# Digraph mixes as products of fp16 halves, delta turned by a transfer, and VectorE operands held in PSUM

## The reference

```
u     = h @ h.T / sqrt(384)
delta = softmax(u) * adj
attn  = delta / (delta.sum(-1) + 1e-10)
ctx   = (attn * upper) @ (h @ Wl.T + bl) + diag(attn)[:, None] * (h @ Ws.T + bs) + (attn * lower) @ (h @ Wr.T + br)
h     = relu((ctx - mean) / sqrt(var + 1e-12) * g + beta)
```

## Time and profile before

| | |
|---|---|
| median of 3 runs | 2729.16 us (2726.61 to 2732.68) |
| profiled execution, its own time | 2730.39 us |
| its span, first to last instruction | 2728.5 us |
| PE busy | 2582.3 us (95%) |
| POOL, DVE, ACT busy | 2117.1 (78%), 2077.7 (76%), 2046.5 us (75%) |
| mean granted TensorE clock | 0.986 |

### The profile page before, as it was taken

The page is one execution under the profiler, slowest core; times in us unless marked ns, Lnnn a source line. Parts: engine busy times, 40 slices in busy tenths (PEclk is TensorE's granted clock), DMA queues, the critical chain, the costliest instruction groups (busy, mean ns, idle before and its releaser), DMA issues.

```text
span 2728.5 us, 90881 instructions
## 1 busy us (share of the span) xinstructions
PE 2582.3 (95%) x33728; PEld 1930.4 (71%) x33728; DVE 2077.7 (76%) x7848; ACT 2046.5 (75%) x5716; POOL 2117.1 (78%) x3211
## 2 busy tenths in 40 slices
PE   5899999999999999999999999999999999999995
PEld 4667777776777777777777777777777777777763
DVE  6677877777877777777777777777787777887774
ACT  6667777777777777777777777777777777787775
POOL 6577878778778788778787788888787787887774
PEclk9899999999999999999999999999999999999997
DMA  7734544445444544444454454444454544454433
GB/s 182 164 62 78 90 86 83 91 84 93 81 87 80 91 91 80 90 91 80 87 94 80 88 93 80 90 91 79 88 94 84 86 88 79 85 96 82 78 61 74
DMA packets 809952, 243.18 MB, mean 89 GB/s; under 512 B 768688, under 2 KB 808752, under 8 KB 809520
## 3 DMA queue, kind: packets, MB, share of 16 engines
q1 hardware_dynamic: 801056, 222.42, 45.5%
q10 hardware_dynamic: 8464, 14.94, 1.8%
HBM read 35.92 MB, written 12.58 MB: 18 GB/s over the span
## 4 chain that ended last, share of the span: by engine, by line
PE 45%; POOL 18%; DVE 16%; ACT 7%; DMA 6%; issue 6%; SPq 1%; DVEq 0%; POOLq 0%; ACTq 0%
PE bank L921 7%; PE bank L923 6%; PE bank L922 6%; PE bank L912 5%; PE bank L913 5%; PE bank L914 5%; DMA region<-region 5%; POOL region L717 3%; DVE region L1091 3%; POOL ab L733 3%; PE bank L995 3%; ACT region L832 2%; POOL region L706 2%; PE bank L951 2%; POOL region L733 2%
## 5 line engine op out<-in xcount | busy, mean ns | idle before, releaser
L912 PE MATMUL bank<-region,w_hi 128*128 128x128 f16 x3960 | 686.0, 220 | 35.0 <-DMA region<-region 25.0
L913 PE MATMUL bank<-region,w_hi 128*128 128x128 f16 x3960 | 685.6, 220 | 0.0
L914 PE MATMUL bank<-region,w_lo 128*128 128x128 f16 x3960 | 685.4, 220 | 0.0
L921 PE MATMUL bank<-w_hi,region 128*128 128x384 f16 x1815 | 593.9, 327 | 11.4 <-DMA region<-region 6.1
L923 PE MATMUL bank<-w_hi,region 128*128 128x384 f16 x1815 | 593.2, 327 | 0.0
L922 PE MATMUL bank<-w_lo,region 128*128 128x384 f16 x1815 | 593.1, 327 | 0.0
L717 POOL TENSOR_TENSOR region<-region 128x512 f16<-128x512 f32 x330 | 385.2, 1167 | 220.6 <-ACT region L838 219.2
L832 ACT ACTIVATE region<-region,small 128x128 f32<-128x128 f32 x1320 | 419.8, 390 | 133.1 <-DVE small L1091 73.2
L912 PEld LDWEIGHTS bank<-region,w_hi 128*128 128x128 f16 x3960 | 390.0, 98 | 63.3 <-issue 26.4
L1091 DVE CUSTOM_DVE_ANT_0 region<-bank,mask 128x128 f32<-128x128 f32 x1320 | 304.4, 285 | 134.5 <-PE bank L951 123.2
L913 PEld LDWEIGHTS bank<-region,w_hi 128*128 128x128 f16 x3960 | 389.9, 98 | 23.8 <-issue 16.5
(11 more groups left out here) (229 smaller groups left out, 7795.8 us busy)
## 6 DMA issues: line engine op xcount, KB each, us to landing
region<-region SPq DMA_TRANSPOSE x715, 3.1
last_unit<-w_dram ACTq DMA_DIRECT2D x19, 576.0 KB, 6.0
x<-x_dram SPq DMA_DIRECT2D x55, 192.0 KB, 2.5
out_dram<-region SPq DMA_DIRECT2D x55, 192.0 KB, 2.2
adj<-adj_dram SPq DMA_DIRECT2D x55, 64.0 KB, 2.3
mask<-adj_t_dram SPq DMA_DIRECT2D x55, 64.0 KB, 2.0
rows<-rows_dram ACTq DMA_DIRECT2D x5, 576.0 KB, 4.3
last_unit<-last_unit SPq DMA_TRANSPOSE x117, 3.1
```

The source lines that it names most:

```text
L912: pe.matmul(dst, lhsT=w_hi[:, w, k, cols], rhs=t_hi[u][:, k, :], start=(k == 0), stop=False)
L913: pe.matmul(dst, lhsT=w_hi[:, w, k, cols], rhs=t_lo[u][:, k, :], start=False, stop=False)
L914: last = pe.matmul(dst, lhsT=w_lo[:, w, k, cols], rhs=t_hi[u][:, k, :], start=False, stop=(k == DT - 1))
L921: pe.matmul(dst, lhsT=t_hi[u][:, k, :], rhs=w_hi[:, w, k, :], start=(k == 0), stop=False)
```

## The change

- Delta: `delta_di` writes its product into the second quarter of the same bank that holds u. `sums` makes the reciprocal of the row sum (a power of -1) in place of the column of 1e-12. ScalarE `delta` writes delta x reciprocal as fp16 into SBUF (the high half), VectorE `delta_low` writes the rest as fp16 (the low half), and takes the diagonal from the bank. The bank is held until then.
- The turn: SP starts a DMA transpose of both halves (128x256 fp16), and POOL `turn_delta` multiplies the turned halves by the two triangles in one instruction (128x512 fp16 out). PE's transpose and VectorE's triangles go.
- The sides: projections 9, 11, 12, 14 go the way that q and k of layer 0 go: VectorE `add_bias` from PSUM into `z` with the bias row, ScalarE a high fp16 half, POOL `low` the low half. POOL `bias` remains for 10 and 13 (the self term). The right side's `add_bias` waits for the left side's `low`, as both use `z`.
- `mix` 2 and 3: six fp16 matmuls of 384 columns each in place of two in fp32.
- Operands of VectorE: `u_gcn` masks left into SBUF and right in its bank, and adds those; `divide` keeps its reciprocals, and for layer 0 also its result, in the last attention bank, from which `residual` 0 reads; a column of `inner` 0 and 1 moves into the mix bank. The attention banks of steps 2 and 5 are so held until `residual` 0 and `divide` 1.
- `PERIOD`, `SHIFTED` and the wished times in `PARTS` are new, so the order of parts on every engine is another one.

```diff
-PERIOD = 20.1080
+PERIOD = 22.1046
...
-    (PE, "mix", 2): (-138.244, 1.340, 1.570, ((VECTOR, "turn_delta", 0), (POOL, "bias", 9), (POOL, "bias", 10), (POOL, "bias", 11)), ()),
...
-           "u_di": lambda k: (VECTOR, "delta_di", k), "turn_delta": lambda k: (VECTOR, "turn_delta", k),
+           "u_di": lambda k: (VECTOR, "delta_low", k),
...
+            def delta_turn(i, layer):
+                u = i % UNITS
+                sp.wait_ge(*mixed_out.at(i, "low delta", layer))
+                sp.dma_start_transpose(delta_t[u], delta_hl[u].rearrange("p a n -> p (a n)")).then_inc(landed.of(i), 16)
...
-                pool.tensor_scalar(col(u, EPS), col(u, DENOM), col(u, DENOM), 1e-12, ALU.mult, ALU.mult).then_inc(gpsimd_done.of(i), 1)
+                pool.tensor_tensor(col(u, INVERSE), col(u, DENOM), constant(MINUS_ONE), ALU.pow).then_inc(gpsimd_done.of(i), 1)
+
+            def turn_delta(i, layer):
+                u = i % UNITS
+                pool.wait_ge(*landed.at(i, "delta", layer))
+                pool.tensor_tensor(triangles[u], delta_t[u].unsqueeze(1).broadcast_to([128, 2, 2, N]),
+                                   tri[:, :, :].unsqueeze(2).broadcast_to([128, 2, 2, N]), ALU.mult).then_inc(gpsimd_done.of(i), 1)
...
+            def high_delta(i, layer):
+                u = i % UNITS
+                act.wait_ge(*gpsimd_done.at(i, "row scale", layer))
+                act.activation(delta_hl[u][:, 0, :], delta_of(i, layer), ACT.Copy, scale=col(u, INVERSE)).then_inc(scalar_done.of(i), 1)
...
-                    pe.matmul(made[:, 0:D], lhsT=triangles[u][:, 0, :], rhs=proj[u][0], start=True, stop=False)
-                    pe.matmul(made[:, 0:D], lhsT=triangles[u][:, 1, :], rhs=proj[u][2], start=False, stop=True)\
-                      .then_inc(multiplied.of(i), 1)
+                    dst = made[:, 0:D]
+                    for side, w in enumerate((left, right)):
+                        high, low = (triangles[u][:, side, n, :] for n in range(2))
+                        h = side_of(u, w)
+                        pe.matmul(dst, lhsT=high, rhs=h[:, 0, :], start=(side == 0), stop=False)
+                        pe.matmul(dst, lhsT=high, rhs=h[:, 1, :], start=False, stop=False)
+                        last = pe.matmul(dst, lhsT=low, rhs=h[:, 0, :], start=False, stop=(side == 1))
+                    last.then_inc(multiplied.of(i), 1)
...
+                    if w in SIDES[1::2]:
+                        dve.wait_ge(*low_of_shifted.at(i, "made", w - 2))
...
-                dve.tensor_tensor(u_pair[u], bank("u_gcn", layer, i)[:, 0:2 * N].rearrange("p (a n) -> p a n", n=N), mask_pair[u], ALU.mult)\
-                   .then_inc(numbers.of(i), 1)
-                dve.wait_ge(*numbers.at(i, "masked", layer))
-                dve.tensor_tensor(e_of(i, "u_gcn", layer), u_pair[u][:, 0, :], u_pair[u][:, 1, :], ALU.add).then_inc(mixed_out.of(i), 1)
+                left, right = (bank("u_gcn", layer, i)[:, n * N:(n + 1) * N] for n in range(2))
+                dve.tensor_tensor(u_left[u], left, mask_pair[u][:, 0, :], ALU.mult).then_inc(numbers.of(i), 1)
+                dve.tensor_tensor(right, right, mask_pair[u][:, 1, :], ALU.mult).then_inc(numbers.of(i), 1)
+                dve.wait_ge(*numbers.at(i, "right masked", layer))
+                dve.tensor_tensor(e_of(i, "u_gcn", layer), right, u_left[u], ALU.add).then_inc(mixed_out.of(i), 1)
...
-                dve.tensor_tensor_reduce(out=score[u][:, 2, :], in0=turned, in1=ident, scale=1.0, scalar=0.0, op0=ALU.mult,
-                                         op1=ALU.add, accum_out=col(u, DIAGONAL)).then_inc(numbers.of(i), 1)
-                dve.tensor_tensor(triangles[u], turned.unsqueeze(1).broadcast_to([128, 2, N]), tri[:, 0:2, :], ALU.mult)\
+            def delta_low(i, layer):
+                u = i % UNITS
+                dve.wait_ge(*scalar_done.at(i, "high delta", layer))
+                dve.scalar_tensor_tensor(delta_hl[u][:, 1, :], delta_of(i, layer), col(u, INVERSE), delta_hl[u][:, 0, :], ALU.mult, ALU.subtract)\
                    .then_inc(mixed_out.of(i), 1)
+                dve.tensor_tensor_reduce(out=delta_of(i, layer, 2), in0=delta_of(i, layer), in1=ident, scale=col(u, INVERSE), scalar=0.0,
+                                         op0=ALU.mult, op1=ALU.add, accum_out=col(u, DIAGONAL)).then_inc(numbers.of(i), 1)
```

More of the change, by code:

```diff
@@ L96 @@
 PARTS = {
[L97 to L108, removed]
@@ L115 @@
[L115 to L127, removed]
@@ L128 @@
[L128 to L133, removed]
@@ L140 @@
[L140 to L145, removed]
@@ L146 @@
[L146 to L150, removed]
-    (SCALAR, "project", 4): (-221.269, 0.370, 0.570, ((PE, "project", 4),), ()),
-    (SCALAR, "scores", 1): (-218.374, 1.920, 2.100, ((VECTOR, "scores", 1), (SYNC, "scores", 0)), ()),
@@ new lines @@
+    (VECTOR, "delta_low", 0): (-416.412, 0.480, 0.460, ((SCALAR, "delta", 0),), ()),
+    (SCALAR, "spread", 1): (-411.268, 0.830, 0.950, ((VECTOR, "residual", 1),), ()),
+    (VECTOR, "delta_gcn", 1): (-405.252, 0.199, 0.407, ((SCALAR, "u_gcn", 1),), ()),
+    (SCALAR, "u_gcn", 0): (-399.740, 0.200, 0.474, ((VECTOR, "u_gcn", 0),), ()),
+    (SYNC, "scores", 0): (-393.049, 1.240, 4.000, ((POOL, "scores", 0),), ()),
+    (SCALAR, "project", 4): (-373.084, 0.370, 0.570, ((PE, "project", 4),), ()),
@@ new lines @@
+    (VECTOR, "inner", 2): (-261.273, 0.560, 0.720, ((PE, "mix", 2), (POOL, "bias", 10), (VECTOR, "delta_low", 0)), ()),
+    (VECTOR, "scores", 0): (-259.672, 0.850, 0.420, ((PE, "scores", 0), (VECTOR, "masks", 0)), ()),
+    (SYNC, "store", 0): (-259.643, 0.500, 2.300, ((SCALAR, "norm", 3),), ()),
+    (POOL, "bias_x", 0): (-258.884, 0.961, 1.245, ((POOL, "turn", 0),), ()),
+    (VECTOR, "add_bias", 14): (-251.016, 0.460, 0.560, ((PE, "project", 14), (POOL, "low", 12)), ()),
+    (SCALAR, "scores", 3): (-247.039, 1.860, 2.040, ((VECTOR, "scores", 3),), ()),
@@ new lines @@
+    (POOL, "low", 1): (-210.639, 0.880, 1.130, ((SCALAR, "project", 1),), ()),
+    (POOL, "scores", 5): (-206.377, 1.150, 1.420, ((SCALAR, "scores", 5),), ()),
+    (SCALAR, "project", 2): (-194.812, 0.370, 0.570, ((PE, "project", 2),), ()),
+    (SCALAR, "spread", 2): (-192.378, 0.830, 0.950, ((VECTOR, "residual", 2),), ()),
+    (POOL, "turn", 1): (-186.922, 0.869, 1.111, ((SCALAR, "turn", 1),), ()),
+    (POOL, "scores", 1): (-181.495, 1.150, 1.420, ((SCALAR, "scores", 1),), ()),
+    (PE, "mix", 1): (-180.864, 0.680, 0.900, ((POOL, "bias", 8), (VECTOR, "delta_gcn", 1)), ()),
@@ new lines @@
+    (SCALAR, "project", 8): (-171.019, 0.370, 0.570, ((PE, "project", 8),), ()),
+    (POOL, "scores", 0): (-164.621, 1.150, 1.420, ((SCALAR, "scores", 0),), ()),
+    (PE, "project", 1): (-157.654, 1.513, 1.710, ((SYNC, "turn", 0),), ()),
+    (SCALAR, "scores", 0): (-157.583, 1.860, 2.040, ((VECTOR, "scores", 0),), ()),
+    (VECTOR, "add_bias", 11): (-153.616, 0.460, 0.560, ((PE, "project", 11), (POOL, "low", 9)), ()),
+    (VECTOR, "residual", 0): (-153.245, 0.480, 0.620, ((VECTOR, "divide", 0), (POOL, "bias_x", 0)), ()),
@@ new lines @@
+    (PE, "project", 0): (-137.817, 1.513, 1.710, ((SYNC, "turn", 0),), ()),
+    (PE, "project", 2): (-135.670, 1.466, 1.660, ((SYNC, "turn", 0),), ()),
+    (PE, "u_gcn", 0): (-132.902, 1.012, 1.270, ((VECTOR, "project", 3), (VECTOR, "project", 4)), ()),
+    (POOL, "turn_delta", 1): (-128.858, 1.120, 1.360, ((SYNC, "delta", 1),), ()),
+    (POOL, "low", 14): (-124.385, 0.880, 1.120, ((SCALAR, "project", 14),), ()),
+    (PE, "scores", 1): (-124.135, 0.360, 0.610, ((SCALAR, "scores", 0),), ()),
@@ new lines @@
+    (SCALAR, "norm", 0): (-93.502, 0.599, 0.740, ((POOL, "residual", 0),), ()),
+    (PE, "mix", 0): (-91.468, 0.680, 0.900, ((POOL, "bias", 5), (VECTOR, "delta_gcn", 0)), ()),
+    (VECTOR, "project", 3): (-91.365, 0.465, 0.743, ((SCALAR, "project", 3),), ()),
+    (POOL, "bias", 13): (-88.411, 0.955, 1.090, ((SCALAR, "project", 13),), ()),
+    (SCALAR, "turn", 4): (-87.378, 0.412, 0.600, ((VECTOR, "gain", 2),), ()),
+    (SCALAR, "u_gcn", 1): (-86.373, 0.200, 0.474, ((VECTOR, "u_gcn", 1),), ()),
@@ new lines @@
+    (PE, "u_di", 0): (-63.186, 0.512, 0.720, ((SYNC, "turn", 3),), ()),
+    (PE, "project", 9): (-61.360, 1.466, 1.660, ((SYNC, "turn", 3),), ()),
+    (PE, "u_di", 1): (-58.852, 0.512, 0.720, ((SYNC, "turn", 4),), ()),
+    (PE, "project", 11): (-58.065, 1.466, 1.660, ((SYNC, "turn", 3),), ()),
+    (VECTOR, "inner", 3): (-57.170, 0.560, 0.720, ((PE, "mix", 3), (POOL, "bias", 13), (VECTOR, "delta_low", 1)), ()),
+    (PE, "project", 10): (-56.460, 1.466, 1.660, ((SYNC, "turn", 3),), ()),
+    (PE, "mix", 2): (-54.977, 0.975, 1.250, ((POOL, "turn_delta", 0), (POOL, "low", 9), (POOL, "low", 11)), ()),
@@ L361, in plan @@
         for w in ROW_OF:
-            comes_after(((POOL, "bias", w), i), ((SCALAR, "load_rows", piece_of(ROW_OF[w])), 0))
```

(14 more changed lines are left out.)

422 lines of the change are left out of this document (221 added, 201 removed), and 60 rows, old and new, of the table SHIFTED.

## The result

2647.5 us (2643.5 to 2650.0) against 2730.6 us before on the same chips: a ratio of 0.9696, 95% interval 0.9679 to 0.9713. That is 83 us less, where 2684 us (45 us less) had been forecast, with 2655 as the lower end of the range.

A forecast was written before the change was run, and what follows sets the result against it. PE's own work was taken to set the pace, 97% busy in the long stretch. 2730.4 - 68.5 (PE) + 20 (returning waits) + 3 (drain) - 1.2 (profile to median) gave 2684 us, range 2655 to 2716.

The forecast's parts named there:

- PE, removed and added: Digraph mixes: fp16 matmuls save 0.365 us each, the dropped transpose 0.17; 1.07 us a unit, 68.5 us in 64 units.
- a microsecond less of PE per unit is worth 64 us: Middle stretch: PE's own work sets the pace, so its savings count fully unless another engine takes its place.
- VectorE's operands: `u_gcn`, `divide`, `residual` 0: VectorE shortens by 0.04 each, 0.31 and 0.18 us; POOL's few tenths a unit left in range.
- rival 3: Relief larger than load: without VectorE's lock waits PE's idle time halves, 2628 us; at most some 15 us, 2648; chance 0.04.
- What comes back: PE's waits grow as other engines fill: 0 to 52 us by scaling with POOL's free time; 20 taken.
- POOL: Bias additions go, `low` and triangle products come: +2.4 us a unit, from 80% to 88% busy, fullest behind PE.
- Rival 1: POOL becomes the bound beside PE: the full 52 us or more comes back, 2708 to 2724, say 2715; chance 0.12.
- VectorE's sum: New `add_bias` and `delta_low`, minus triangles and shorter waits: net +1.3 us a unit, 32.0 to 33.3, 83% busy.
- The chain: Delta to mix in a layer: from 1.0 to 5.3 us through five queues, transfer 2.8 us; hidden in the middle.
- rival 2: The transfer's turn comes late and PE waits at the mix: slower, 2789 us at 1 us per mix; chance 0.09.
- Ends: Drain, where PE is partly idle and longer chains are seen: 0 to 8 us, 3 taken.
- Rival 4: Nothing changes, since PE's time isn't the pace; nearly excluded by PE 97% busy; chance 0.03 with cases between 1 and 2.

The follow-up runs named there:

- run 7: Changed kernel, POOL's triangle product doubled: 2762.6 us. Old kernel with operands in PSUM, two POOL bias additions cut: 2679.1 us; also without the mixes' second fp32 matmul: 2660.8 us.

## Why the prediction was wrong, step by step

- *PE, removed and added.* The size of the work was right: 0.97 us a mix as forecast, no transpose, PE's busy time down by 1.18 us a unit for 1.07; a unit took 39.66 us, where 40.3 to 40.8 was forecast. **A first step that failed is "a microsecond less of PE per unit is worth 64 us".** I read it off 97% busy and short waits. In an unchanged order 83 us less gave 13 us, and 0 with operands in PSUM. With the mix and its new order together, but VectorE's operands in SBUF, the change gives 17 us (2730.6 to 2713.5); on top of the operands in PSUM 37 us (2684.3 to 2647.5). That is what came of the 68.5, or of the 45 that my sum left of them after +20 and +3, and only with an order made for it; the old wishes with the new code give 2846. How much of the 17 or 37 is PE's work and how much the order, no run parts.
- *VectorE's operands.* **The second step that failed, and the one that put the result outside the range: I costed them at nothing and left them "in the range".** They are worth 51 us in the old kernel and 66 in the new, the larger half of the result, while the mix came out 8 to 28 us below its 45. I had the row (a median of 306, a mean of 482) and the rule that went with it, and turned it into VectorE's busy time only. Two things I did not do: count the small instructions of `divide`, which can wait as long as the long ones, and price the delay for what stands behind them. My rival 3, the relief larger than the load, was the nearest to the truth, with a chance of 0.04 and a cap of 15 us that had no row under it. That its 2648 is the measured number is luck: it adds PE's busy time at -68.5, its idle time at -15 and the ends at +3, and what was measured is -75, -26 and +19.
- *What comes back.* +20 was a scaling of PE's idle time by POOL's. PE's idle time fell instead. In the run with operands in SBUF it did rise by 0.46 us a unit, so the worry was sound for the mix alone; the operands paid for it. I had treated the two halves of the change as one load.
- *POOL.* +2.4 us a unit forecast, +1.68 measured, and +2.34 with VectorE's operands in SBUF. The triangle product took 1.157, so the upper of my two prices was right; the difference is the end of POOL's own waits (the bias addition 1000 for 1060), which I had left in the range. POOL runs at 87%, as forecast, and PE waits for it 0.6 us in the whole stretch. Rival 1 as a wait of PE for POOL isn't there; POOL as a partner in the pace is (run 7).
- *VectorE's sum.* +1.3 forecast, +0.57 measured, and +1.99 with the operands in SBUF, where my terms without the relief of 0.57 make 1.9. So the work was priced rightly and the relief too low, 1.43 for 0.57: the small instructions again. (`delta_low` took 0.348 where I took 0.288.)
- *The chain and rival 2.* The transfer landed in 2.4 us (median), less than the 2.8 assumed, and PE's waits for transfers fell. The longer chain is hidden in the middle. The rule in VectorE: DVE Perf Modes of the Trainium skill, to transpose on TensorE where PSUM will do, spoke for a loss that didn't come; nothing here set the two transposes against each other with the rest equal.
- *Ends.* +3 forecast, +19 measured over start and drain. By the same subtraction the kernel before with only the longer holds has ends of 101 us for 89, so some 12 of the 19 may belong to the held banks and the order they make, and not to the longer chain; no run shows it apart.
- *Rival 4*, PE's time isn't the pace, I took to be "nearly excluded". It was true in the sense that counts.

## What to carry to other kernels

A high busy share says that an engine has no room for more, not that taking work from it gives time back: in a kernel whose engines all run at 75 to 97% in one planned order, try both signs, a cut and a ballast, before a saving is priced at one for one. A VectorE instruction with operands in SBUF whose mean or median is far above its minimum has waited; count the twelve-element ones too, and try one operand in PSUM when a bank is at hand. The wait isn't its price, which depends on the place: 0.38 us more of mean wait at `u_gcn`'s addition cost 3 us here, 0.2 to 0.3 at the small ones of `divide`, with the product behind them, 43. And where an order is planned for given costs, compare code only under one order: half a percent on one planning number was worth more here than the whole change.

## What the runs showed that I had not expected

- VectorE's instructions with one operand in PSUM are constant to some ns over 2500 us (299/299/300, 553/553/555, 546/548/558), with POOL busy 87% beside them; with both in SBUF the same work took up to 1.1, 1.3 and 1.5 us in the kernel before.
- It goes both ways: POOL's busy time fell by 0.52 us a unit when VectorE's operands left SBUF, though none of POOL's instructions changed. SBUF — State Buffer of the Trainium skill (Who interferes with whom) has the lock as exclusive, and by that these runs agree. `L1156` has one input, in SBUF, with its output there too, and waited as well (419 ns for 116 with the output in PSUM).
- 148 us more POOL work cost 115 us, 62 us more PE work 51 us, 72 us more VectorE work 25 us, while 83 us less PE work gave 0 to 13 and some 100 us less POOL work 5.
